# Where the rounding steps of a four-bit feed-forward layer are kept: PSUM or SBUF

## What is computed

```
def fp4_quant_dequant(x):
    xb = x.reshape(shape[:-1] + (shape[-1] // 16, 16))
    scale = max(|xb|, axis=-1) / 6.0
    scale = maximum(scale, 1e-12)
    xn = xb / scale
    idx = searchsorted(_MID, |xn|)          # _MID = 0.25 0.75 1.25 1.75 2.5 3.5 5
    q = _GRID[idx] * sign(xn) * scale       # _GRID = 0 0.5 1 1.5 2 3 4 6
fp4_linear(x, w) = quant(x) @ quant(w).T
h = silu(fp4_linear(x, w_gate)) * fp4_linear(x, w_up)
out = fp4_linear(h, w_down)
```

## Time and profile before

| what | value |
|---|---|
| median of 3 runs | 1350.44 us (1349.83 to 1356.36) |
| span of the profiled execution | 1349.0 us |
| PE busy | 1132.4 us, 84% |
| PE weight load busy | 681.7 us, 51% |
| DVE busy | 902.5 us, 67% |
| ACT busy | 487.8 us, 36% |
| POOL busy | 540.3 us, 40% |
| mean granted clock of TensorE | 0.945 of full speed |

### The profile page before, as it was taken

The page is one execution under the profiler, slowest core; times in us unless marked ns, Lnnn a source line. Parts: engine busy times, 40 slices in busy tenths (PEclk is TensorE's granted clock), DMA queues, the critical chain, the costliest instruction groups (busy, mean ns, idle before and its releaser), DMA issues.

```text
span 1349.0 us, 16030 instructions
## 1 busy us (share of the span) xinstructions
PE 1132.4 (84%) x4801; PEld 681.7 (51%) x4801; DVE 902.5 (67%) x2031; ACT 487.8 (36%) x958; POOL 540.3 (40%) x453
## 2 busy tenths in 40 slices
PE   3899999964867768999999899999988883698992
PEld 1444444432457445555555555555565552466672
DVE  5788888888889685777777577777746664333220
ACT  3544544445534563222222322222232221255451
POOL 4788888984346234000000000000002667277776
PEclk9899999986989987999999999999999996799997
DMA  4422222200000031000071000000001122565632
GB/s 137 125 60 61 61 61 61 61 0 1 0 1 1 1 145 74 24 24 16 23 282 63 1 16 24 23 16 16 10 8 32 52 87 91 127 133 96 112 43 22
DMA packets 66191, 73.86 MB, mean 55 GB/s; under 512 B 10223, under 2 KB 44369, under 8 KB 65617
## 3 DMA queue, kind: packets, MB, share of 16 engines
q1 hardware_dynamic: 52369, 64.46, 15.4%
q0 software_dynamic: 13504, 8.62, 4.5%
q10 hardware_dynamic: 256, 0.03, 0.0%
HBM read 29.73 MB, written 28.02 MB: 43 GB/s over the span
## 4 chain that ended last, share of the span: by engine, by line
PE 61%; DVE 16%; issue 9%; POOL 7%; ACT 5%; SPq 1%; DMA 1%; POOLq 0%; ACTq 0%; DVEq 0%
PE banks L1696 41%; PE banks L1568 7%; POOL expert_in_scratch L1115 2%; PE banks L1731 2%; PE banks L1500 2%; PE banks L1501 2%; PE banks L1509 1%; POOL arena L1021 1%; DVE arena L754 1%; DVE banks L747 1%; DVE arena L1983 1%; POOL powers L1129 1%; POOL arena L1028 1%; DVE arena L2014 1%; POOL out_dram L1153 1%
## 5 line engine op out<-in xcount | busy, mean ns | idle before, releaser
L1696 PE MATMUL banks<-arena 128*128 128x128 f32 (+3 forms) x1480 | 380.8, 394 | 14.5 <-ACT arena L1465 9.3
L1696 PEld LDWEIGHTS banks<-arena 128*128 128x128 f32 (+1 forms) x1480 | 202.5, 190 | 89.4 <-issue 62.6
L1568 PE MATMUL banks<-arena,ident 128*128 128x512 f32 x368 | 172.4, 600 | 10.8 <-DVE arena L2014 9.8
L1153 POOL DMA_INDIRECT out_dram<-arena x80 | 126.0, 1575 | 67.2 <-issue 37.4
L1021 POOL TENSOR_TENSOR arena<-arena 128x512 f32<-128x512 f32 x96 | 112.2, 1194 | 14.3 <-ACT arena L1194 14.3
L1568 PEld LDWEIGHTS banks<-arena,ident 128*128 128x128 f32 x368 | 66.9, 191 | 87.4 <-issue 64.0
L1111 POOL IOTA arena<- 128x32 f32 x1 | 0.2, 218 | 261.2 <-DVE ttt_val_w L2260 261.2
L1387 ACT ACTIVATE arena<-banks 128x512 f32<-128x512 f32 x64 | 38.2, 597 | 175.6 <-PE banks L1731 175.6
L2014 DVE TENSOR_TENSOR arena<-arena,banks 128x512 f32<-128x512 f32 x152 | 96.2, 676 | 0.5 <-PE banks L1568 0.5
L1696 PEld LDWEIGHTS banks<-ttt_proj_w,arena 128*128 128x128 f32 x512 | 67.8, 194 | 31.7 <-issue 29.2
L1028 POOL TENSOR_TENSOR arena<-arena 128x512 f32<-128x512 f32 x64 | 81.3, 1270 | 5.0
(11 more groups left out here) (350 smaller groups left out, 2135.2 us busy)
## 6 DMA issues: line engine op xcount, KB each, us to landing
arena<-arena SPq DMA_DIRECT2D x64, 224.0 KB
arena<-expert_in_scratch SPq DMA_DIRECT2D x14, 589.5 KB
expert_in_scratch<-arena SPq DMA_DIRECT2D x4, 1244.5 KB
expert_in_scratch<-arena SPq DMA_DIRECT2D x5, 982.5 KB
arena<-kT_scratch SPq DMA_DIRECT2D x16, 256.0 KB, 2.7
arena<-k_scratch SPq DMA_DIRECT2D x16, 256.0 KB, 2.7
arena<-in_L_ffn_W_dram SPq DMA_DIRECT2D x16, 256.0 KB
kT_scratch<-arena SPq DMA_DIRECT2D x8, 256.0 KB
```

Source lines behind the costliest of these rows:

```text
L1153: pool.indirect_dma_start(out=out_rows_dram, out_offset=bass.IndirectOffsetOnAxis(ap=y_at[0:r, s, j:j + 1], axis=0), in_=yo[0:r, q, j % 4, ...
L1568: m = nc.tensor.matmul(bank[ACC[b % 2]][:], ident[:], src, start=first, stop=last)
L1696: return nc.tensor.matmul(out_, lhsT, rhs, start=start, stop=stop)
```

## The change

```diff
         def steps_of(k):
-            c, nb = shape_of(k)
-            return by_tiles_of(bank[6]) if k < NB else banks[:, 2:2 + TPB, 0:16 * nb]
+            return by_tiles_of(levels(k))
```

## The result

| | before | after |
|---|---|---|
| median of the runs made side by side | 1353.4 us (4 runs) | 1375.4 us (4 runs) |
| ratio, with its 95% interval | | 1.0161 (1.0131 to 1.0191) |
| span of the profiled execution | 1349.0 us | 1371.6 us |

The account below looks back on a forecast made before the run. DVE was taken to set the pace of groups 8 to 15. Groups 8 to 15 (+15.5) and groups 0 to 7 (+3.7) made +19.2 us, so 1369.6 us against the median of 1350.44; range 1363 to 1376.

Parts of the forecast that it names:

- DVE and POOL take turns, and the one that waits gets 0.15 us of its own time for free: Where both use SBUF, the waiter runs when the other ends, some 0.15 us already done; a round 9.96 for 7.34.
- The mask's rate doubles: Mask written to SBUF, all 16 groups: 0.89 us instead of 1.62 for 1408 elements, 0.43 instead of 0.69 for 512.
- Add and less cost nothing by themselves: Add and less with both inputs in SBUF: 1.61 us alone, what they take now with a PSUM input; change zero.
- The 65 ns an instruction: Skill page's estimated saving on 32 add and less instructions, 2.1 us at most; the prediction took zero.
- Groups 8 to 15: +15.5: Last product's stretch: six rounds of 9.96 for 7.34 cost 15.7, group 8's mask -0.7, group 15 0.5; sum 15.5 us.
- The last group, put at +0.5: Group 15: POOL and mask start together, the add ends 1.66 late, mostly covered; 0.5 us, ends 0 and 1.7.
- Group 0 +0.5, groups 2 to 6 +1.3: Beside gate, up and silu: group 0's add ends 0.5 late; masks 0.39 late five times, 1.3 taken of 1.95.
- Group 7 +1.9: Group 7's mask waits for group 8's 2.59 us division and ends at 366.57 instead of 364.65: +1.9 us.
- the clock, but for the last product: Upper end of range: TensorE could stand at 1.2 GHz in the last product, 438.19 to 445.04, at up to 4 us.
- The rivals: Three alternatives: rival 1, rival 2, and a third where nobody waits, only the mask's faster rate left: 1344; its chance 0.05.
- rival 1: Mask keeps one element at a time and never waits for POOL; groups 8 to 15 pay 13.6; 1366; chance 0.10.
- rival 2: DVE keeps its turn from add to less, POOL waits for both; a round 10.05 us; 1370; chance 0.07.

Follow-up runs that it names:

- half_pool: Changed kernel with POOL's divisions and multiplications back of groups 10 to 15 half as long (704 elements); one run, trace only: a round 7.68 us, less 2.69.
- h_only: Kernel before with only the steps of groups 8 to 15 moved to SBUF, those of groups 0 to 7 left in PSUM; ratio 1.0123 (1.0092 to 1.0155).
- not7: Changed kernel with group 7's steps in PSUM; one run, trace only: mask of group 8 comes 15.61 us after that of group 7.
- x_only: Kernel before with only the steps of groups 0 to 7 moved to SBUF, those of groups 8 to 15 left in PSUM; ratio 1.0053 (1.0033 to 1.0072).
- warm: Changed kernel plus 14 useless matmuls on TensorE before group 6's first gate product; one run, trace only: 0.7 us gained, 1.3 expected.
- warm9: Changed kernel plus nine useless matmuls before group 6's first gate product; one run, trace only: 17.46 us from group 7's mask to group 8's.
- psum_sum: Changed kernel with ScalarE's small values and the add's sum in PSUM, so add and less have one SBUF input each; ratio 1.0063 (1.0043 to 1.0082).
- reorder: psum_sum with DVE's order changed, and maxima and reciprocals in PSUM from group 10 on; ratio 0.9986 (0.9968 to 1.0003) to the kernel before.
- reorder2: reorder with group 8's small values in SBUF and group 15 rounded as in the kernel before (steps in PSUM); ratio 0.9977 (0.9967 to 0.9986).
- half_pool_psum: Kernel before with POOL's instructions of groups 10 to 15 half as long; one run, trace only: rounds 7.33 to 7.34 us.

## Why the prediction was right, point by point

- **DVE and POOL take turns, and the one that waits gets 0.15 us of its own time for free**: right to 0.01 us. Less was put at 3.89 (5.54 - 1.65) and takes 3.89, the division at 3.9 and takes 3.90, masks of groups 9 to 14 at 1.97, rounds at 9.96 and they are 9.97. The three places in the first half of layer 0 were enough for it, and half_pool, at another length, came out at the forecast number too.
- **The mask's rate doubles**: right, 0.42 and 0.89 where nothing is beside it (0.43 and 0.89 forecast), -0.7 in group 8.
- **Add and less cost nothing by themselves**: right; both take 1.62 or 1.63 with two SBUF inputs and nothing beside them, and the same with one in PSUM. The prediction had only compared a 512-element instruction of another line with the mask; this is the like with the like. The 65 ns an instruction, an estimate from the Trainium skill's page "VectorE: DVE Perf Modes", section "The TRN2 errata — SBUF-src ops pay a fixed extra latency per instruction", don't show here either, at 1408 elements; 88-element instructions do show 0.05 us (last section).
- **Groups 8 to 15: +15.5**: 15.4 in the changed kernel, 14.6 in h_only. From the mask of group 8 to that of group 15 the two agree (64.13 and 64.14 us); the 0.8 arises behind it, where TensorE's first six matmuls on group 14 take 1.49 us at the lower clock in the changed kernel (the line at 452.96 above), and 0.87 in h_only. not7, whose instructions from group 8 on are those of h_only, has the 1.45 and the 0.8 too, so it is not the change's as such. That the clock is the cause was not tried. By terms: six rounds and group 8's mask make 15.1 at the mask of group 15, as forecast (15.0). The last group, put at +0.5, is -0.4 in h_only and +0.3 in the changed kernel. Its 1.66 is covered almost whole, since TensorE is less behind: in h_only it starts on group 14 2.62 us after that mask, and 3.11 in the kernel before.
- **Group 0 +0.5, groups 2 to 6 +1.3**: 0.48, and 1.46 in x_only, all of it in groups 3 to 6; group 2 is wholly covered.
- **Group 7 +1.9**: the term that was mis-sized. The mask's wait is as forecast (2.60 us), but what followed from it was not thought through: the product of the next tile comes 1.9 us late, TensorE rests meanwhile, its clock falls to 1.2 GHz, and four pairs of matmuls run slow: 3.18 in all. The text named the clock, but for the last product, the one of group 15; there the granted clock is 1.00 in the changed kernel, and the slow stretch lies before it, between 450 and 455 us.
- **The rivals**: all three fell. Masks with a neighbour take 1.97 and not 1.62, POOL does get in between add and less, and everybody waits. By the sum alone, rival 1 (1366) and rival 2 (1370) could not have been told from the forecast; the durations do it.
- The total was 19.2 and the two spans lie 22.6 apart: 1.3 are the clock behind group 7, 0.6 the clock at group 2 (below), and 1.5 lie outside the part. So the change itself costs between 19.8 us (x_only and h_only together) and 20.6 (21.1 less the 0.57 at group 2) in this part. That the sum comes as close as 19.2 is in part luck: group 7 was short by 1.3, and group 15 long by 0.9 in h_only, by 0.2 in the changed kernel. The six rounds, four fifths of the sum, owe nothing to luck.

## What to carry to other kernels

Where VectorE and GpSimd work side by side, what counts is not how long an instruction takes alone, but whether it asks for SBUF twice: two inputs there, or a tensor_scalar that runs at the double rate from SBUF to SBUF. For the instructions tried here one operand in PSUM was enough to let both engines run at once, and the price of moving it could be read in advance from places of the same trace where the two met: the one that waits ends at the other's end plus its own time, less some 0.15 us. Such waits don't show as idle time but as longer instructions, so a "busy" engine has to be compared by the mean of one instruction, and a late instruction on a path that feeds TensorE can cost its clock on top.

## What the runs showed that had not been expected

- **In these traces the clock rose at one of two moments.** From the mask of group 2 to that of group 3 it is 7.81 or 7.82 us in the kernel before, x_only, h_only, not7, half_pool, warm and warm9, and 8.39 to 8.42 in the changed kernel, psum_sum and reorder (8.47 in reorder2), but also 8.38 in half_pool_psum, whose instructions up to there are those of the kernel before. In the windows view the changed kernel has a granted clock of 0.55 from 328 to 332 us, the kernel before 1.00 from 327 to 331, behind the same four gate and up products. So these 0.57 us are not the change's; a single pair of traces would have laid them to it.
- **Work of no use can save time**: nine matmuls on a resting TensorE gave 1.33 us, fourteen only 0.7.
- The two small tensor_scalar instructions with an operand in PSUM took 0.25 us instead of 0.20 for 88 elements. For 1408 elements no such difference showed.
